# A dense row of a mixture of experts routed behind the scans of a state-space layer, and its neighbours' queues reordered

## The reference

```
x = x + scan(norm(x)); x = x + mixture(norm(x)); x = x + conv(norm(x)); x = x + mixture(norm(x))

scan:     u = x w_in; dt, B, C from u; per channel d and time s, with 16 states:
          h = exp(dt A) h + sum_d(dt A B u);  y = sum_n(h C) + Dp u
mixture:  probs = softmax(x Wr + br); gate, idx = max, argmax over 8 experts
          pos = rank of the token among those of its expert, in order over all 4 rows
          kept if pos < 512;  out = gate (relu(gate x W1[idx] + b1) W2[idx] + b2)
conv:     three streams of x w_in with 3 taps each; v = s2 * s0, a long convolution of v
          with a filter that a small MLP makes (silu, silu, linear), times s0, times w_out
```

## Time and profile before

| | us |
|---|---|
| median of 3 runs (all: 515.61, 516.10, 526.08) | 516.1 |
| the profiled execution | 517.27 |
| its span, first to last instruction | 516.0 |
| busy: PE, DVE, ACT, POOL | 341.4, 349.6, 228.9, 308.2 |
| scans on DVE, 64 | 140.9 |
| mean granted clock of TensorE | 0.787 |

### The profile page before, as it was taken

One profiled execution on the slowest core, in us unless ns is written; L12 is line 12 of the kernel. 1 busy time (PEld: TensorE's weight loads), 2 busy tenths in 40 slices (PEclk: granted clock), 3 DMA queues, 4 the chain that ended last, 5 costly groups with the idle time before them and its releaser, 6 DMA issues.

```text
span 516.0 us, 5443 instructions
## 1 busy us (share of the span) xinstructions
PE 341.4 (66%) x1535; PEld 188.2 (36%) x1535; DVE 349.6 (68%) x798; ACT 228.9 (44%) x368; POOL 308.2 (60%) x218
## 2 busy tenths in 40 slices
PE   4887844586948494898738889562889754408560
PEld 3333310322402240345424556320567644306340
DVE  4897599999999999996511363716678775407350
ACT  2876556256536364834202364342883411105440
POOL 2242069699989697994571066572533555644766
PEclk9988875589796586697875999856888977557885
DMA  7034040790000010010310321013011021222200
GB/s 216 4 107 133 6 122 0 222 360 0 1 0 0 3 41 0 1 41 23 104 51 17 95 73 55 10 32 100 0 42 41 24 67 37 89 95 91 82 25 12
DMA packets 29849, 31.24 MB, mean 61 GB/s; under 512 B 5518, under 2 KB 22964, under 8 KB 29820
## 3 DMA queue, kind: packets, MB, share of 16 engines
q1 hardware_dynamic: 25180, 24.35, 15.6%
q0 software_dynamic: 3840, 5.84, 3.5%
q10 hardware_dynamic: 800, 0.71, 0.5%
HBM read 13.91 MB, written 19.12 MB: 64 GB/s over the span
## 4 chain that ended last, share of the span: by engine, by line
PE 28%; DVE 26%; issue 20%; POOL 8%; another core or an unknown queue 5%; DVEq 5%; ACT 5%; DMA 1%; ACTq 1%; POOLq 0%; SPq 0%
DVE states L839 12%; POOL slots L1087 3%; PE ps L1193 3%; PE ps L1741 2%; PE ps L1209 2%; POOL out L1505 2%; PE ps L1671 2%; DVE reply L1482 2%; PE ps L682 2%; PE ps L697 2%; PE ps L1113 2%; PE ps L553 1%; POOL c_v L1709 1%; PE ps L580 1%
## 5 line engine op out<-in xcount | busy, mean ns | idle before, releaser
L822 POOL TENSOR_TENSOR states<-states,c_rows 128x1024 f32<-128x1024 f32 x62 | 147.3, 2411 | 32.1 <-DVE states L839 31.9
L839 DVE TENSOR_TENSOR_SCAN states<-ps,inp 128x1024 f32<-128x1024 f32 x64 | 140.9, 2266 | 0.6 <-ACT ps L796 0.4
L796 ACT ACTIVATE ps<-ps,bias_p,scale_p 128x1024 f32<-128x1024 f32 x64 | 74.8, 1176 | 72.7 <-PE ps L682 72.5
L682 PE MATMUL ps<-stack,sel 96*128 96x512 bf16 x128 | 50.0, 485 | 49.3 <-DVE states L839 49.3
L1087 POOL DMA_INDIRECT slots<-x,put x56 | 55.3, 987 | 41.4 <-DVE put L1081 26.5
L1505 POOL DMA_INDIRECT answers<-reply,home x32 | 31.5, 985 | 39.7 <-DVE reply L1482 32.1
L1505 POOL DMA_INDIRECT out<-reply,home x32 | 31.6, 986 | 22.5 <-DVE reply L1482 13.9
L682 PEld LDWEIGHTS ps<-stack,sel 96*128 96x128 bf16 x128 | 8.9, 105 | 87.8 <-DVE states L839 80.7
L1482 DVE SCALAR_TENSOR_TENSOR reply<-ps,rows,kept 128x128 f32<-128x128 f32 x64 | 18.6, 345 | 30.8 <-remote 17.2
L697 PE MATMUL ps<-states,red 128*32 128x512 f32 x256 | 36.0, 671 | 1.7 <-POOL states L822 1.7
L1697 DVE SCALAR_TENSOR_TENSOR c_s<-c_u,c_w_tap,c_s 128x1024 f32<-128x1024 f32 x16 | 19.8, 1280 | 19.3 <-ACT c_s L1688 19.0
(11 more groups left out here) (201 smaller groups left out, 690.7 us busy)
## 6 DMA issues: line engine op xcount, KB each, us to landing
slots<-zero SPq DMA_DIRECT2D x8, 528.0 KB
rows<-slots SPq DMA_DIRECT2D x16, 264.0 KB
steps<-part SPq DMA_DIRECT2D x4, 768.0 KB, 3.2
stack<-steps SPq DMA_DIRECT2D x12, 256.0 KB, 4.1
out<-x SPq DMA_DIRECT2D x4, 512.0 KB
x<-in_x SPq DMA_DIRECT2D x3, 512.0 KB, 5.7
answers<-x SPq DMA_DIRECT2D x3, 512.0 KB
x<-answers SPq DMA_DIRECT2D x3, 512.0 KB, 5.7
```

The source lines that it names most:

```text
L682: last = pe.matmul(bank(ps, slot(b, u) + q), sel[0:PARTS * QUARTER, (g % QG) * P:(g % QG + 1) * P], stack[:, g // QG, bass.ds(b * SEQ + q ...
L796: act.activation(bank(ps, slot(b, u), 2), bank(ps, slot(b, u), 2), ACT.Exp, scale=m["scale_p"][:, group(u):group(u) + 1], bias=m["bias_p"] ...
L822: eng.tensor_tensor(h[:, u * SEQ:(u + 1) * SEQ], h[:, u * SEQ:(u + 1) * SEQ], c_rows[:, b * SEQ:(b + 1) * SEQ], ALU.mult).then_inc(done, 1)
L839: dve.tensor_tensor_scan(h[:, u * SEQ:(u + 1) * SEQ], bank(ps, slot(b, u), 2), inp[:, b * SEQ:(b + 1) * SEQ], 0.0, ALU.mult, ALU.add).then ...
```

## The change

The dense row is routed after the last scan, as the first of the four: its gates (`gates`) right after its choice, and its places, of which it needs only which tokens are kept (`keep`), behind row 1's. Its normalisation and transposes follow there. The number column of `x` is written between two scans of row 0. Group 9 is on VectorE in all rows. The filter's weights are loaded at the last scan's end, and `time0` is cleared then, before the scatters; the first filter layer comes ahead of the dense steps, which are 12 before the experts instead of 13. In the conv layer row 1's statistics come before row 0's taps, row 0 shares banks 2 and 3 for its long convolution, and its part of the pipeline follows the pattern of the others. A part of the late buffers is allotted after the conv layer's, and the filter's weights take memory that the scans use.

```diff
-ON_DVE = ((9,), (9,), (), ())
+ON_DVE = (9,)
...
+    m["all_open"] = 2 * QG * (BATCH - 1) + 1
...
-                if (b, u) in early["vector"]:
-                    early["vector"][b, u](dve)
+                if b == 0 and u == 8:
+                    dve.tensor_scalar(x[:, :, NUMBER], const[:, C_TOKEN:C_TOKEN + TILES], 1.0 - TOKENS, None, ALU.add)
...
+    def gates(self, dve, n):
+        m, q, b = self.m, n % 2, n % BATCH
+        tiles = slice(b * BT, (b + 1) * BT)
+        column = lambda c: m["x"][:, tiles, c]
+        need(dve, self.exp, n + 1)
+        dve.tensor_reduce(m["total"][:, :], m["prob"][:, q, :, :], AX, ALU.add)
+        dve.drain()
+        dve.reciprocal(column(GATE), m["total"][:, :])
+        dve.drain()
+        dve.tensor_tensor(column(FACTOR), column(GATE), m["rstd"][:, self.use(n), tiles], ALU.mult)
+        dve.drain()
+        dve.tensor_tensor(column(SHIFT), column(FACTOR), m["neg_mean"][:, self.use(n), tiles], ALU.mult).then_inc(self.placed, 1)
+    def keep(self, dve, n):
+        m, q, b = self.m, n % 2, n % BATCH
+        need(dve, self.count_psum, n + 1)
+        dve.tensor_tensor(m["cum"][:, :, :], self.ps[:, self.counts(n):self.counts(n) + BT * EXPERTS].rearrange("p (i e) -> p i e", e=EXPERTS),
+                          m["onehot"][:, q, :, :], ALU.mult).then_inc(self.kept, 1)
+        dve.drain()
+        dve.tensor_reduce(m["pos"][:, :], m["cum"][:, :, :], AX, ALU.add)
+        dve.drain()
+        dve.scalar_tensor_tensor(out=m["kept_gate"][:, :], in0=m["pos"][:, :], scalar=float(CAP), in1=m["x"][:, b * BT:(b + 1) * BT, GATE],
+                                 op0=ALU.is_lt, op1=ALU.mult)
+        dve.drain()
...
         m = self.m
         need(act, self.router.placed, DENSE + 1)
+        need(act, m["scanned"], BATCH * GROUPS)
...
-    def clear(self, pool):
-        pool.memset(self.time0[:, :], 0.0)
+    def clear_time(self, pool):
+        need(pool, self.m["scanned"], BATCH * GROUPS)
+        need(pool, self.m["summed"], self.m["all_open"])
+        pool.memset(self.time0[:, :], 0.0).then_inc(self.cleared, 1)
+    def clear_edges(self, pool):
         pool.memset(self.u[:, :, :, 0:self.PAD], 0.0).then_inc(self.cleared, 1)
-    def y_bank(self, b):
-        return 6 if b == DENSE else self.U0
...
             pe.wait_ge(self.weights_in, self.n_weights)
             need(pe, self.cleared, 1)
+            need(pe, self.kept, 1)
             pe.matmul(self.layer_psum(0), self.w1[:, :], self.time0[:, :], start=True, stop=True).then_inc(self.mlp_psum, 1)
...
+        need(act, self.cleared, 2)
...
-        if b != DENSE:
-            need(pe, self.u_done, min(2 * b + 3, 2 * BATCH - 1))
+        need(pe, self.u_done, min(2 * b + 3, 2 * BATCH - 1))
         need(pe, self.y_read, b)
-        at = self.y_bank(b) * HALF
+        at = self.Y * HALF
...
-    def first_statistics(dve):
-        dve.memset(m["prior"][:, :, :], 0.0)
-        router.statistics(dve, DENSE)
-    def first_choice(dve):
-        dve.wait_ge(m["router_in"], 16 * 2)
-        router.choose(dve, DENSE)
-    m["early_row"]["vector"] = {(2, 1): first_statistics, (2, 8): first_choice, (3, 2): lambda dve: router.place(dve, DENSE)}
-    m["early_row"]["tensor"] = {(2, 11): lambda pe: router.count(pe, DENSE)}
-    m["early_row"]["scalar"] = {(2, 5): lambda act: router.row_deviations(act, DENSE), (2, 11): router.take_count,
-                                (2, 12): lambda act: router.probabilities(act, DENSE), (2, 14): dense.far_away}
+    m["early_row"]["scalar"] = {(2, 14): dense.far_away}
     @plan.on("sync")
     def _(sp):
+        need(sp, m["scanned"], BATCH * GROUPS)
+        need(sp, m["summed"], m["all_open"])
+        conv.load(sp)
         for b in range(DENSE + 1, BATCH):
             need(sp, m["x_added"], 2 * b + 2)
             store_rows(sp, m, 0, b)
-        conv.load(sp)
         conv.filter_sync(sp)
         experts.sync(sp, 0)
         experts.fetch(sp)
...
+        router.count(pe, DENSE)
+        m["tail"]["logits"]()
+        dense.turn(pe)
         router.count(pe, 1)
-        dense.first(pe, 0)
-        m["tail"]["logits"]()
-        steps(1, 2)
         m["tail"]["back"]()
+        conv.filter_tensor(pe, 0)
+        steps(0, 2)
         router.count(pe, 2)
         steps(2, 5)
         router.count(pe, 3)
-        steps(5, 7)
-        for layer in range(3):
-            conv.filter_tensor(pe, layer)
-            steps(7 + layer, 8 + layer)
-        steps(10, 13)
+        steps(5, 8)
+        conv.filter_tensor(pe, 1)
+        steps(8, 9)
+        conv.filter_tensor(pe, 2)
+        steps(9, 12)
         conv.toeplitz_tensor(pe)
         need(pe, conv.toep_done, 1)
-        experts.tensor(pe, 0, lambda e: steps(12 + e, 13 + e) if 12 + e <= dense.STEPS else None)
-        conv.transpose(pe, 0)
-        conv.streams(pe, 0)
-        conv.v_transpose(pe, 0)
-        conv.long_conv(pe, 0)
...
+        experts.tensor(pe, 0, lambda e: steps(11 + e, 12 + e) if 11 + e <= dense.STEPS else None)
+        row_steps((lambda b: conv.output(pe, b), 2),
+                  (lambda b: conv.transpose(pe, b), 0), (lambda b: conv.streams(pe, b), 0),
+                  (lambda b: conv.v_transpose(pe, b), 1), (lambda b: router.count(pe, second(b)), 3),
+                  (lambda b: conv.long_conv(pe, b), 1),
+                  (lambda b: router.transpose(pe, second(b), conv.x_done, b + 1), 2), (lambda b: router.logits(pe, second(b)), 2))
         experts.tensor(pe, 1)
     @plan.on("scalar")
...
+        router.row_deviations(act, DENSE)
+        router.probabilities(act, DENSE)
+        m["tail"]["take_sums"]()
+        dense.normalize(act, range(BT))
+        router.row_deviations(act, 1)
+        m["tail"]["take_logits"]()
         for h in range(2):
             dense.take_rows(act, h)
-        router.row_deviations(act, 1)
-        dense.take_mask(act, 0)
         router.probabilities(act, 1)
-        dense.take_mask(act, 1)
-        m["tail"]["take_sums"]()
+        for h in range(2):
+            dense.take_mask(act, h)
+        m["tail"]["take_rows"]()
         hide(0, 1)
-        m["tail"]["take_logits"]()
+        router.row_deviations(act, 2)
         hide(1, 2)
-        router.row_deviations(act, 2)
-        m["tail"]["take_rows"]()
...
-        hide(10, 13)
+        hide(10, 12)
         conv.toeplitz_scalar(act)
-        experts.scalar(act, 0, lambda e: hide(12 + e, 13 + e) if 12 + e < dense.STEPS else None)
+        experts.scalar(act, 0, lambda e: hide(11 + e, 12 + e) if 11 + e < dense.STEPS else None)
         conv.early_deviations(act)
         conv.normalize(act, 0)
-        conv.copy(act, 0)
-        conv.take_streams(act, 0)
-        conv.first_tap(act, 0)
-        conv.v_copy(act, 0)
-        conv.normalize(act, 1)
-        for k in range(1, BATCH + 3):
+        for k in range(BATCH + 3):
             step(k, lambda b: conv.copy(act, b))
-            step(k + 1, lambda b: conv.normalize(act, b))
+            if k > 0:
+                step(k + 1, lambda b: conv.normalize(act, b))
             step(k, lambda b: conv.take_streams(act, b))
-            if k > 1:
-                step(k - 1, lambda b: conv.v_copy(act, b))
+            step(k - 1, lambda b: conv.v_copy(act, b))
             step(k - 3, lambda b: router.probabilities(act, second(b)))
             step(k, lambda b: conv.first_tap(act, b))
+            if k == 0:
+                conv.normalize(act, 1)
...
     @plan.on("vector")
     def _(dve):
-        dve.tensor_scalar(m["x"][:, :, NUMBER], m["const"][:, C_TOKEN:C_TOKEN + TILES], 1.0 - TOKENS, None, ALU.add)
-        for b in range(DENSE + 1, BATCH):
+        dve.wait_ge(m["router_in"], 16 * 2)
+        for b in range(BATCH):
             router.statistics(dve, b)
+            if b == DENSE:
+                dve.memset(m["prior"][:, :, :], 0.0)
             router.choose(dve, b)
-            router.place(dve, b)
+            if b == DENSE:
+                router.gates(dve, b)
+            else:
+                router.place(dve, b)
+            if b == DENSE + 1:
+                router.keep(dve, DENSE)
...
         def merge(e):
-            if e == 4:
+            if e == 5:
                 dense.merge(dve)
-            if e == 5:
+            if e == 6:
                 statistics(dve, m, 1, DENSE).then_inc(conv.moments, 1)
         experts.vector(dve, 0, merge)
...
         conv.early_shifts(dve)
+        fetched(1)
         conv.taps(dve, 0)
-        for b in range(DENSE + 1, BATCH):
+        for b in range(2, BATCH):
             fetched(b)
         conv.gate_y(dve, 0)
...
     @plan.on("gpsimd")
     def _(pool):
         pool.wait_ge(m["prepared"], PREPARED)
+        conv.clear_time(pool)
         for b in range(DENSE + 1, BATCH):
             router.scatter(pool, b)
         need(pool, m["x_added"], 2 * BATCH)
-        conv.clear(pool)
+        conv.clear_edges(pool)
...
         conv.bias(pool, 0)
+        conv_rstd(1)
         conv.product(pool, 0)
```

(2 more changed lines are left out.)

72 lines of the change are left out of this document (24 added, 48 removed).

## The result

The kernel after takes **507.95 us** (median of 4 runs, 506.83 to 509.57); the kernel before, run beside it, 519.88 (4 runs, 515.61 to 526.08). The ratio is **0.985**, 95% interval [0.980, 0.990]: about 1.5% faster, less than the 2% that a measurement here tells from no change. The forecast was 511, in a range of 503 to 521; against the 516.1 it started from that is a ratio of 0.990. The profiled execution took 506.83 with a span of 505.6; the one before 517.27 with 516.0.

The account below looks back on a forecast made before the run. It took VectorE's scans as the bound up to 228.77, then the filter as deciding. The profiled 517.3, less 7 at the experts' start, plus 1 and 1, gave 512.3; with the median 1.2 lower, 511, range 503 to 521.

Parts of the forecast that it names:

- TensorE's start among the experts: TensorE starts the experts 7 us earlier, near 285.9; bounds 1 us later to 13 earlier.
- Scans: Scan stage on VectorE: three interruptions go (12.3 us), products cost 2.2 and the column 2.0; ends 8.1 us earlier, at 220.7.
- number column: Column operation moved between two scans of row 0: costs 2.0 us there, bounds 0.2 and 2.2.
- To the first scatter: From the scans' end to row 1's first scatter: 16.6 us instead of 10.4, so the scatter comes 1.9 us earlier.
- The column behind the scans: Number column gone from behind the scans, ahead of the first scatter: 1.86 us less.
- Last scatter: End of the token scatters: 1.9 us earlier, at 271.1, with the pattern of waits kept; about 4 us either way.
- Row loads: Loads of the experts' rows issued 1.5 + 1.9 + 1.6 = 5 us earlier, near 280, with no stand on `time0`.
- Given back among the experts: The dense step taken out is done between experts instead: +1 us (0 to 2.3).
- Convolution: New order in the convolution: row 0's gate late, row 1's taps only about 1 us later; +1 us (-2.4 to +4).
- Loads early, stores behind them: Filter loads issued at the scans' end, rows 1 and 2 stored behind them: costs nothing, being covered by 15 us of routing.
- rival B: TensorE's dense steps under the scatters become the bound; experts start 7 us later, 525 us (522 to 529); chance 0.12.
- Rival A: The filter leaves the path: row loads 12.5 us earlier, directly behind the scatters; 505.6 us, down to 502; chance 0.2.

Follow-up runs that it names:

- e4: The kernel after, unchanged, run again for a second trace: 508.76 us.
- e7: The kernel after with group 9's products of rows 2 and 3 back on GpSimd and the number column back behind the scans: 512.0 us (one run).
- e2: The kernel after with `time0` cleared behind the scatters and the first filter layer back behind dense step 7: 512.97 us, ratio 0.989.
- e3: The kernel after with the filter's and convolution's weight loads back behind the stores of rows 1 to 3: 506.38 us, ratio 0.974.
- e5: The kernel after, with GpSimd waiting until a row's scatters have landed before the next row's (two waits): 503.63 us, ratio 0.968.
- e6: The kernel after with rows 2 and 3 routed together and the filter's three layers spread between them: 508.77 us, ratio 0.979.
- e8: The kernel after with the convolution's order as in the kernel before: 505.45 us (one run).
- e12: The same kernel as e9, on a third chip: 500.22 us, ratio 0.974.
- e9: The kernel after with e5's waits, row 3's deviations and probabilities earlier on ScalarE, its count and the filter one dense step earlier; another chip: 485.82 us, ratio 0.973.
- e10: The same kernel as e8, on another chip: 482.38 us, ratio 0.971.
- e11: The kernel before with only the two GpSimd waits of e5, on the chip of e9 and e10: 501.99 us, ratio 1.003.
- e1: The kernel before with only `time0` cleared ahead of the scatters, the last buffers allocated to allow it: 517.89 us, ratio 0.991.

## Why the prediction held, and where it did not

The net gain was forecast at 5 us on the profiled execution. In the first trace it is 5.3 once the 5.1 us of the start are taken out; between traces with the same start (before and e4) the spans differ by 9.0, and the runs side by side by 1.5%. The order of events held: scans shorter, half of it given back ahead of the first scatter, row loads earlier, some of it lost among the experts. That the first trace comes so near to 5 is luck: TensorE's start among the experts was 3.7 us earlier than forecast, and 4.7 us more than forecast were lost behind it. By steps:

- **Scans**: forecast 8.1 earlier, measured 10.8. The mis-sized term is the number column, +2.0: it cost 0.0 (e7). I had priced the operation by its own duration and not asked what it pushes. With the products' 2.1 (forecast 2.2), the interruptions were worth 12.9 against 12.3.
- **To the first scatter**: forecast 16.6, measured 15.8. ScalarE's normalisation cost 1.0, where 1.2 was forecast.
- **The column behind the scans**: counted at 1.86 less. Had it stayed there, it would have cost up to 7.17 (e7), since the scans now end with other products running. L464 took 1.23 in after and 3.08 in e7, a difference of most of a product of GpSimd. The Trainium skill, page "SBUF — State Buffer", section "SBUF: two separate sides", has the two engines lock a shared port pair, the loser blocked for a whole instruction, for VectorE's operations in a two-port mode or with two inputs in SBUF. These two numbers agree with it, while 7.17 us is three products long, and the same operation took 1.96 in before with products running too; whether this operation, with one input, is of the kind that the page means, no run shows. Taking none of the rule for the sum was near enough for the products (2.1) and missed what the column pushes.
- **Last scatter**: forecast 1.9 earlier, measured 0.9 in one trace and 5.9 in the other (e4, start for start). The prediction had kept the pattern of the waits; the two executions of the same kernel had two different ones.
- **Row loads**: forecast 5 earlier, measured 8.0 (e4 9.8). e2 prices the filter's part at 4.6 to 6.4, where the prediction had 1.5 + 1.6. **The first rows on VectorE** came 8.0 earlier, TensorE's start 10.7 (forecast 7).
- **Given back among the experts**: forecast 1, measured 5.7 from TensorE's start to the last answer (57.2 us against 51.6), but only 3.2 in e4. GpSimd stood five times there, 4.0, 1.8, 3.4, 2.9 and 1.3 us, together 13.3; in before its stands come to 8.1, in e4 to 11.5. TensorE had a granted clock of 0.66 in the 20 us from its start in the first trace, and of 1.00 in before and e4; the prediction had nothing on it. Late completions don't account for the loss: before had 15.1 us of such waits in this stage and after less than 5. In e3, e5, e6, e8 and e12, whose code of this stage is after's, it took 50.6 to 51.9, that is nothing given back; in e2 53.3, and in e7, with a clock of 0.74 in those 20 us, 58.9. So most of the 5.7 belongs to the execution and not to the change. The two traces with the lowest clock there have the longest stages, but e4's 54.7 came at 1.00, and what makes the difference was not tested.
- **Convolution**: forecast +1, measured -0.3 in the first trace and +0.3 in e4, and 0 on the other chip (e9, e10); e8 stands apart. Row 0's gate was late by 4.8 (forecast 6 to 9) and row 1's taps not, as argued.
- **Loads early, stores behind them**: costed at nothing, and e3 agrees. With the cover gone the layer waited for the loads, as the prediction says, but that cost nothing that shows.

The 20 us from TensorE's start among the experts, in before, after and e4 (columns as above, the granted clock third from the end):

```profile
292.83:312.83 20.00, 16.69 (x89) 10.92 (x89) 9.15 (x35) 11.73 (x28) 11.43 (x12) 1.00 0.21 62
```
```profile
277.02:297.02 20.00, 17.93 (x66) 11.81 (x67) 10.29 (x41) 9.08 (x22) 8.02 (x9) 0.66 0.16 48
```
```profile
280.41:300.41 20.00, 15.99 (x86) 10.54 (x87) 11.39 (x45) 10.34 (x24) 11.42 (x12) 1.00 0.22 63
```

The range of 503 to 521 was said to end at rival B's low end, but that is 522; nothing hangs on it.

Rival A, the filter leaving the path, was given 0.2 for 12.5 us. It did not happen where the result was measured. On the chip without late completions the loads did go out directly behind the scatters: e10 took 31.7 us from the first scatter to the row loads, where e11, with the filter as before and two short pauses, took 45.6, so 13.9 less, and the loads went out 1.4 us after the last scatter. The rival hung on why completions came late. I made it hang on TensorE's stand on `time0`, and e1 refutes that: without this stand the filter layer reached VectorE 10.2 us after it was issued. TensorE did stand in that time, but for ScalarE, which waited for a late completion itself.

Rival B did not come. Its mechanism showed in e6, where TensorE began with the experts 13 us after the rows were there. By the rule on the clock that the prediction took from the Trainium skill the first dense steps run at the lower level. The traces show both: the first one ran at a granted clock of 1.00 in after and of 0.50 in e4, and neither made TensorE the bound.

**What stays open**: what delays TensorE's completions. Under the scatters they went with GpSimd's runs of indirect DMAs on every chip that had them, and in e5 the first one ended with the run of 8. But in e4 one ended 1.4 us before a run did (265.41), in e1 one in the middle of a run of 16 (258.07, the run from 247.99 to 267.89), and on one chip a run of the same length delays nothing. No experiment here separates these, nor shows that TensorE had in truth done a matmul where its record stands.

## What to carry to other kernels

Before a wait that the profile cannot name is priced, look whether it is there in a second execution and on a second chip: here it went with whether the change gave 1.5% or, on the chip without such waits, 2.9% (e10, with the old order of the convolution). Keep what the next long stage hangs on (row 3's deviations) out of the queue behind an engine that waits for such a completion, and do not let one removed wait stand for a gain until the same data is seen to arrive earlier (e1). Don't price a small operation beside GpSimd's products by one record of it: the column's took 1.82, 1.96 and 7.17 us, and the first of these cost nothing in sum. Before a loss in a stage behind the change is put down to it, look at the same stage in a second execution.

## What the runs showed of the hardware that was not expected

- At least three chips with 8 to 16 waits put down to "remote" in each trace, and one with none, where the kernel before took 498.6 us and not 516 to 520.
- The first 60 us in two ways, granted clock 0.91 or 1.00, 5 us apart.
- One operation of 128x32 on VectorE at 1.82, 1.96 and 7.17 us, at three places beside GpSimd's products.
- The experts' stage of one kernel, from TensorE's start to the last answer, in 57.2 and 54.7 us, with a granted clock of 0.66 and 1.00 in its first 20 us.
